# Attention mix in blocks of four key steps, ScalarE drains moved ahead of a block, out projections by chunks of two tiles, and the low parts of the transposed x formed from PSUM

## What is computed

```python
h = layernorm(x) * (1 + ca) + sa
q = h @ Wq.T                                   # 8 heads of 64
kv = h @ Wkv_down.T; k = kv @ Wk_up.T; v = kv @ Wv_up.T
attn = softmax(q @ k.T / 8)
x = x + ga * ((attn @ v) @ Wo.T)
h = layernorm(x) * (1 + cb) + sb
x = x + gb * (h @ weight.T + pooled(h) @ disha)
```

## Time and profile before

| | us |
|---|---|
| median of 3 runs | 3203.18 (3201.83 to 3203.7) |
| the profiled execution, its own time | 3202.91 |
| its span, first to last instruction | 3201.1 |
| PE busy | 3155.7 (99%) |
| POOL busy | 2594.8 (81%) |
| DVE busy | 2198.4 (69%) |
| ACT busy | 1708.8 (53%) |

### The profile page before, as it was taken

How to read it: one execution, slowest core, us unless ns; L and a number is a source line. 1 busy time by engine, 2 the same in 40 slices (tenths; PEclk the granted TensorE clock), 3 DMA queues, 4 the chain that set the end, 5 groups by cost and what they waited for, 6 DMA issues and landing times. The chain is left out here.

```text
span 3201.1 us, 45110 instructions
## 1 busy us (share of the span) xinstructions
PE 3155.7 (99%) x15394; PEld 1916.2 (60%) x15394; DVE 2198.4 (69%) x2530; ACT 1708.8 (53%) x3209; POOL 2594.8 (81%) x1521
## 2 busy tenths in 40 slices
PE   7999999999999999999999999999999999999997
PEld 5555656656566665666666566665666666666555
DVE  6567676776767767677776777767677676776664
ACT  3555555554555555555555555555555455555544
POOL 3888788887878878788887888878878787887786
PEclk9999999999999999999999999999999999999999
DMA  2111111211112111111111111111120121211111
GB/s 82 37 41 60 47 57 34 76 35 47 57 47 67 34 57 54 47 57 44 47 54 56 58 34 54 57 47 57 43 71 31 48 67 38 67 37 48 47 50 41
DMA packets 161252, 162.91 MB, mean 51 GB/s; under 512 B 58112, under 2 KB 109440, under 8 KB 161024
## 3 DMA queue, kind: packets, MB, share of 16 engines
q1 hardware_dynamic: 161024, 160.03, 15.3%
HBM read 74.40 MB, written 17.33 MB: 29 GB/s over the span
## 5 line engine op out<-in xcount | busy, mean ns | idle before, releaser
L962 POOL TENSOR_TENSOR prob_sum<-prob_sum,probs 128x1024 f32<-128x1024 f32 x768 | 1882.6, 2451 | 243.9 <-ACT probs L803 189.4
L1108 DVE TENSOR_REDUCE neg_max<-ps_max 128x1 f32<-128x1024 f32 x1024 | 1247.6, 1220 | 753.9 <-PE ps_max L634 748.0
L803 ACT ACTIVATE probs<-ps_score 128x512 f32<-128x512 f32 x2048 | 1113.3, 598 | 969.2 <-PE ps_score L611 958.3
L588 PE MATMUL ps_mix<-probs,values 128*64 128x512 f32 x4096 | 991.6, 605 | 0.0
L609 PE MATMUL ps_score<-query,key_hi 128*128 128x512 f32 x2048 | 873.8, 427 | 1.1 <-ACT probs L803 1.1
L611 PE MATMUL ps_score<-query_m,key_lo 128*128 128x512 f32 x2048 | 805.1, 393 | 0.0
L634 PE MATMUL ps_max<-key_hi,query 128*128 128x512 f32 x2048 | 640.7, 394 | 5.0 <-DVE neg_max L1108 3.5
L609 PEld LDWEIGHTS ps_score<-query,key_hi 128*128 128x128 f32 x2048 | 384.7, 188 | 326.8 <-issue 247.0
L588 PEld LDWEIGHTS ps_mix<-probs,values 128*64 128x64 f32 x4096 | 248.4, 136 | 477.8 <-issue 477.0
L962 POOL TENSOR_TENSOR prob_sum<-probs 128x1024 f32<-128x1024 f32 x128 | 328.5, 2567 | 209.2 <-ACT probs L803 208.9
L634 PEld LDWEIGHTS ps_max<-key_hi,query 128*128 128x128 f32 x2048 | 383.8, 188 | 96.6 <-DVE neg_max L1108 5.6
(11 more groups left out here) (197 smaller groups left out, 2832.8 us busy)
## 6 DMA issues: line engine op xcount, KB each, us to landing
query_m<-query SPq DMA_DIRECT2D x128, 512.0 KB, 3.2
recip<-recip_scratch SPq DMA_DIRECT2D x254, 128.0 KB, 2.9
x_in<-in_L_attn_x_dram SPq DMA_DIRECT2D x32, 512.0 KB, 3.9
x_mid<-in_L_attn_x_dram SPq DMA_DIRECT2D x64, 256.0 KB, 4.5
out_dram<-x_mid SPq DMA_DIRECT2D x64, 256.0 KB, 2.2
denoms<-recip SPq DMA_DIRECT2D x508, 1.0 KB, 1.7
gates<-gates_scratch SPq DMA_DIRECT2D x16, 256.0 KB, 4.1
query_m<-max_row SPq DMA_DIRECT2D x128, 4.0 KB
```

What stands on the lines that cost most here:

```text
L588: last = nc.tensor.matmul(ps_mix[j * R:j * R + R, :], values[par][:, k, :], probs[:, s % RING, j * HALF:(j + 1) * HALF], start=(k == 0), s ...
L803: nc.scalar.activation(probs[:, s % RING, half * HALF:(half + 1) * HALF], ps_score[half], ACT.Exp, scale=SCALE).then_inc(exps_done, 1)
L962: nc.gpsimd.tensor_tensor(out=total[:, :], in0=before, in1=probs[:, s % RING, :], op=ALU.add).then_inc(adds_done, 1)
L1108: nc.vector.tensor_reduce(neg_max[:, m:m + 1], ps_max[m % 2][:, :], AX_X, ALU.max, negate=True).then_inc(maxima_done, 1)
```

## The change

- MIXED goes from 2 to 4: the mixes stand in blocks of four steps, at the steps with s % 4 == 1, and RING goes from 4 to 6 to hold the probabilities so long. The ring now runs on from batch to batch.
- PLAN is written anew. Pieces whose ACT drain is long stand at s % 4 == 0, pieces that DVE drains and a few transposes at s % 4 == 2. What ACT drains at s % 4 == 2 it drains after the exponentials of the next step. `mixed_hi`, `h2_split` and the high parts of weights stand at s % 4 == 1, the steps with a block. MIX_LAG is 4, and a `denominator` stands at NT*(i+1)+1, `max_row` at STEPS-NT+5+NT*i.
- `out_proj` has 4 pieces of two tiles each.
- For `norm_t` ACT's second pass reads the high part from SBUF and makes shift - high of it, and DVE forms the low part as PSUM * scale + (shift - high) in one SCALAR_TENSOR_TENSOR, which also drains the bank.
- The two copies of `mixed` are replaced by one tile of 11 half rows that consecutive batches share, and the copy-out of a group waits, in groups 2 and 4 to 7, for a `mixed_split` of the batch before.

```diff
-RING = 4
+RING = 6
-SPREAD_LAG, RECIP_LAG, OUT_LAG, BACK_LAG, MIX_LAG = 1, 2, 2, 3, 5
-MIXED = 2
+SPREAD_LAG, RECIP_LAG, OUT_LAG, BACK_LAG, MIX_LAG = 1, 2, 2, 3, 4
+MIXED = 4
-AHEAD_LOAD, AHEAD_STATS, AHEAD_APPLY = 44, (48, 49, 50, 51), 53
-NEXT_LOAD, NEXT_STATS, NEXT_APPLY = 61, (0, 1, 2, 3), 4
+AHEAD_LOAD, AHEAD_STATS, AHEAD_APPLY = 22, (29, 33, 37, 41), 43
+NEXT_LOAD, NEXT_STATS, NEXT_APPLY = 47, (1, 1, 1, 1), 2
-OUT_GATES_LOAD, OUT_GATE, OUT_HI, OUT_LO = 44, 52, 54, (56, 59)
-FFN_GATE, FFN_HI, FFN_LO = (1, 8), (3, 9), (3, 11)
+OUT_GATES_LOAD, OUT_GATE, OUT_HI, OUT_LO = 8, 27, 45, (45, 49)
+FFN_GATE, FFN_HI, FFN_LO = (1, 3), (3, 5), (3, 5)
-    "query": (40, 42, 50, 58, STEPS, STEPS + 2, STEPS + 4, STEPS + 6),
-    "norm_t": (8, 10, 16, 18),
-    "latent": (26, 32),
-    "values_t": (54, 60),
-    "mixed_hi": (9, 16, 24, 40),
-    "mixed_lo": (10, 17, 25, 41),
-    "out_proj": (12, 14, 20, 22, 30, 36, 44, 46),
-    "norm2": (16, 25, 38, 49),
-    "norm2_t": (24, 34, 48, 56),
-    "h2_split": (25, 35, 49, 57),
-    "ffn": (28, 38, 52, 62),
+    "query": (32, 36, 40, 44, 48, 52, STEPS, STEPS + 4),
+    "norm_t": (8, 12, 16, 20),
+    "latent": (24, 28),
+    "values_t": (42, 46),
+    "mixed_hi": (9, 13, 17, 25),
+    "mixed_lo": (9, 13, 17, 25),
+    "out_proj": (10, 14, 22, 30),
+    "norm2": (11, 19, 35, 51),
+    "norm2_t": (18, 34, 50, 56),
+    "h2_split": (21, 37, 53, 57),
+    "ffn": (26, 38, 54, 62),
...
-        "max_row": STEPS - NT + 1 + NT * i,
-        "denominator": NT * (i + 1) + 3,
+        "max_row": STEPS - NT + 5 + NT * i,
+        "denominator": NT * (i + 1) + 1,
...
-                        g, j = divmod(i, CT)
-                        need(pe, mixed_split, CHUNKS * b + g + 1)
+                        need(pe, mixed_split, CHUNKS * b + i + 1)
...
-                    for kind, i, b, w in z.at(s):
+                    late = z.has_c and s % MIXED == 2
+                    for kind, i, b, w in z.at(s - 1) * (z.has_c and s % MIXED == 3) + z.at(s) * (not late):
...
-                            for part, done in ((h_hi[:, f, cols], h_hi_done), (h_whole[:, i % 2, :], side_drained[room])):
-                                nc.scalar.activation(part, side, ACT.Identity,
-                                                     scale=mod1[:, f:f + 1], bias=mod1[:, NF + f:NF + f + 1]).then_inc(done, 1)
+                            nc.scalar.activation(h_hi[:, f, cols], side, ACT.Identity,
+                                                 scale=mod1[:, f:f + 1], bias=shift).then_inc(h_hi_done, 1)
+                            need_alone(act, h_hi_done, 2 * (2 * NF * b + i) + 1)
+                            nc.scalar.activation(h_whole[:, i % 2, :], h_hi[:, f, cols].bitcast(F32), ACT.Identity,
+                                                 scale=-1.0, bias=shift).then_inc(h_hi_done, 1)
...
+                            nc.vector.scalar_tensor_tensor(h_lo[:, f, cols], side, mod1[:, f:f + 1], h_whole[:, i % 2, :],
+                                                           ALU.mult, ALU.add).then_inc(side_drained[room], 1)
```

More of the change, by code:

```diff
@@ L291, in adaln_block @@
         prob_total = recip
-        mixed = [sb(f"mixed{i}", [P, PAIRS, T]) for i in range(2)]
+        mixed = sb("mixed", [P, 2 * PAIRS + 3, HALF])
         mixed_hi = sb("mixed_hi", [P, PAIRS, CT * P], F32R)
@@ L654, in side_work @@
                     elif kind == "latent":
-                        need(pe, h_split, 2 * NF * b + NF * (i + 1))
+                        for f in range(NF):
+                            drained(pe, z, "norm_t", NF * i + f)
                         if first(z):
@@ L689, in side_work @@
                             need(pe, w_out_split, len(OUT_LO) * (b + 1))
-                        g, j = divmod(i, CT)
-                        need(pe, mixed_split, CHUNKS * b + g + 1)
+                        need(pe, mixed_split, CHUNKS * b + i + 1)
                         need(pe, side_drained[room], count)
-                        m_hi, m_lo = mixed_parts(z, g)
+                        m_hi, m_lo = mixed_parts(z, i)
                         products = [(mp, wp, p) for p in range(PAIRS)
                                     for mp, wp in ((m_hi, w_out_hi), (m_lo, w_out_hi), (m_hi, w_out_lo))]
-                        for q, (mp, wp, p) in enumerate(products):
-                            last = nc.tensor.matmul(side[:, 0:D], mp[:, p, j * P:(j + 1) * P],
-                                                    wp[:, p, :], start=(q == 0), stop=(q == len(products) - 1))
+                        for j in range(CT):
+                            for q, (mp, wp, p) in enumerate(products):
+                                pair = PAIRS - 1 - p if (1 - z.par) else p
+                                last = nc.tensor.matmul(side[:, j * D:(j + 1) * D], mp[:, p, j * P:(j + 1) * P],
+                                                        wp[:, pair, :], start=(q == 0), stop=(q == len(products) - 1))
                     elif kind == "norm2_t":
@@ L998, in slot @@
                         need(pool, gates_loaded, 16 * (z.c + 1))
[L999 to L1001 removed]
+                        if not z.has_o:
                             for i in range(4):
@@ L1123, in slot @@
                             hi, lo = mixed_parts(z, g)
-                            nc.vector.tensor_tensor(lo, mixed[1 - z.par][:, :, g * CT * P:(g + 1) * CT * P],
+                            nc.vector.tensor_tensor(lo, mixed_chunk(1 - z.par, g),
                                                     hi.bitcast(F32), ALU.subtract).then_inc(mixed_split, 1)
-                    for kind, i, b, w in z.at(s - 1):
-                        if kind == "norm_t":
-                            need(dve, h_hi_done, 2 * NF * b + i + 1)
-                            drained(dve, z, kind, i)
-                            half, f = divmod(i, NF)
-                            cols = slice(half * HALF, (half + 1) * HALF)
-                            nc.vector.tensor_tensor(h_lo[:, f, cols], h_whole[:, i % 2, :], h_hi[:, f, cols].bitcast(F32),
-                                                    ALU.subtract).then_inc(h_split, 1)
-                    if z.has_n and not first(z) and s in NEXT_STATS:
-                        statistics(z.n, 1, NEXT_STATS.index(s))
+                    for i, t in enumerate(NEXT_STATS):
+                        if z.has_n and not first(z) and s == t:
+                            statistics(z.n, 1, i)
                     for i, t in enumerate(AHEAD_STATS):
```

80 lines of the change are left out of this document (48 added, 32 removed).

## The result

The changed kernel takes **3365.59 us** (3358.11 to 3367.59, 4 runs) against 3203.44 (3201.83 to 3204.41): a ratio of 1.0502, 95% interval 1.0484 to 1.0521. Forecast were 3263 and a range up to 3305. The sign and the two large waits were right, the size was 103 us short.

A forecast was written before the change was run, and what follows sets the result against it. PE was taken to bound the kernel, busy 99% of the span. From 3202.9 us, 90 came off for fewer blocks and 150 were added for new PE waits, giving 3263; the range was 3135 to 3305.

The forecast's parts named there:

- the two large waits: New PE idles a batch: 4.3 us before chunk 1's out projection, and 2.4 twice before the feed-forwards.
- Term 1: Edges of mix blocks on PE: 16 instead of 32 blocks a batch, 0.35 us saved each, -90 us in all.
- Term 2 (a): Second chunk of the out projection, step 14: PE waits 4.3 us for `mixed_lo`, delayed by POOL's additions; 0.8 without the port.
- Term 2 (b): Feed-forward of chunks 1 and 2, steps 38 and 54: PE waits 2.4 us for h2's low part, twice, 4.8.
- Term 2 (c): Denominator of group 0, step 9: PE waits 0.9 us (0 to 1.5) for POOL's chain of additions.
- The clock falls in the waits: Rival: matmuls behind the out projection's 4.3 us wait run at a lower clock, 2.3 more a batch, 3298 us; chance 0.12.
- Terms of nothing: Out projections by two tiles, low part of x from PSUM, and ACT's second pass and later drains: no cost expected.
- at most 15 a run: Bound on the cost if cover for the transposes' drain by ACT at three steps a batch were gone; taken as 0.
- The low part of the transposed x from PSUM: DVE operation with one SBUF tensor, 64 times 0.7 us; DVE was said to have room, so priced at nothing.
- A free port: Rival: the port DVE and POOL share is mostly free, so few waits of PE arise, 3138 us; chance 0.20.
- Only (a) bites: Rival: the feed-forward waits mostly hide and the out projection's wait stays, 3191 us, faster by 0.4%; chance 0.12.
- POOL becomes the bound: Rival: POOL's additions no longer fit a batch of 194, further denominators come late, 120 us more, 3380; chance 0.05.

The follow-up runs named there:

- experiment 1: The changed kernel, with DVE multiplying a group's mix by the reciprocals behind `mixed_lo` of the same step instead of ahead of it: 3280.9 us.
- experiment 3: The changed kernel, with POOL's additions 2 to 7 of each group on 32 of 1024 columns and the first adding ones: 3170.67 us.
- experiment 11: The kernel of experiment 2, with DVE's `w_ffn_lo` at step 6 of a slot instead of step 5: 3177.18 us.
- experiment 4: The changed kernel, with useless PE matmuls ahead of its waits, 14 before the second chunk's out projection and 8 before two feed-forwards: 3320.44 us.
- experiment 5: The kernel of experiment 2, with ACT's two exponentials of a step covering only 256 and 384 of 512 columns: 3140.52 us.
- experiment 2: The changed kernel, with DVE multiplying behind both `mixed_lo` and the low part of h2: 3175.46 us, ratio 0.9907 to the kernel before.
- experiment 7: The kernel before, with only the low part of the transposed x formed from PSUM: 3226.33 us.
- experiment 8: The kernel of experiment 2, with PE's two maxima matmuls ahead of the four score matmuls at steps 0 mod 4: 3232.7 us, ratio 1.0086.

## Why the prediction failed, by its own steps

- **Term 1, fewer blocks, -90:** right. 5.63 a batch against 5.6 forecast, and a block of 3.71 against 3.69. The differences of 0.10 and 0.15 between time stamps in the earlier trace rows were enough to read it.
- **Term 2 (a):** right in place and mechanism; an idle of 3.80 and 3.96 between starts for 4.3, and experiments 1 and 3 show both the wait's worth and its cause. The times came out as in the working: counted from the first score matmul of step 10 in the batch shown above, POOL's norm starts at 6.8 (forecast 6.7), its additions at 9.4 and 11.9 (9.4 and 11.9), the multiplication ends at 14.8 (14.9) and `mixed_lo` at 18.1 (18.4). The multiplication had to wait for one addition in flight, `mixed_lo` for the next.
- **Term 2 (b):** right; 2.38 twice, 5.1 between starts for 4.8.
- **Term 2 (c):** absent in the result, for a reason that the term left out: it took PE as undisturbed up to step 9, and PE had already lost 0.75 behind step 5, where `w_ffn_lo` and the multiplication stand next to each other. The working of (c) was right about POOL (0.84 in experiment 11). The time that it named was lost, under another name.
- **First step that failed: the clock as a rival.** The forecast took (a) and (b) at the full clock and gave 0.12 to "The clock falls in the waits". It does, behind the idle of 3.80 in all fourteen batches, and in all but two of them behind one or both of the 2.38 as well. Nothing in the kernel before shows an idle of this size in mid-batch; but the earlier trace rows showed the fall behind 6.99, and none showed that a shorter idle was harmless. Cost: 3.0 in the batch of the sum, 45 us in all (experiment 4); the rival had 2.3 a batch, for (a) alone. The mean clock of 0.979 is the sign that the prediction itself had named for it.
- **Second: "Terms of nothing", ACT's work.** Between blocks of four, steps now follow each other with nothing but scores and maxima on PE, in 20 places a batch. There the weights of the first scores can't be loaded before the exponentials have freed the bank, so the first two score matmuls start up to 0.08 late each. Before, a block or side work stood in these gaps and hid it. 2.2 in the batch of the sum, 35 us in all (experiment 5). The forecast looked at ACT's share of 107 in 200, which says nothing here: what counts is the time from the last score of one step to the first of the next. The one delay that it priced there, "at most 15 a run", was that of the transposes' drain at three steps a batch; the exponentials at the other steps had no term.
- **Third: the ends of the program.** The terms were priced for 15 like batches. The last slot prepares no batch behind it, so PE has less to do beside each step, and the same waits are longer there: 6.34, 3.28 and 4.48 for 3.80 and 2.38 twice, at a lower clock. Why they are longer was not tested by itself; with DVE's order changed (experiment 2) the last slot is 20 shorter. The beginning and the last slot together are 28 longer; the terms gave them -2.
- **Sum.** Of the missing 102 of the span, 72 lie in fourteen batches, 5.1 each: clock 3.0, late scores 2.2, the single reduction 0.75, less 0.9 by which (a), (b) and (c) together were forecast too high (9.06 measured for 10.0). The other 30 lie in the beginning and the last slot. The forecast and the rival of the clock were written as alternatives, although the fall of the clock follows from the waits that the forecast has. That put the top of the range at 3305.
- **"The low part of the transposed x from PSUM" at nothing:** not borne out where it was tested alone, 22 us in the kernel before (experiment 7). DVE had the room; the bank did not.
- **The rivals.** A free port (3138, 0.20) falls with experiment 3: made free, the port gives back 195 us, so in the changed kernel it was not free. (3170.67 and not 3138, since the late scores remain, 35 us.) "Only (a) bites" falls with experiment 1, in which (a) is gone and 72.0 us ahead of L732 stay. "POOL becomes the bound" falls with the profile: POOL is busy for 76% and PE's L699 matmuls wait for it once, 1.0 us.

What is still open: whether 20 late starts could be hidden by side work placed there (experiment 8 moved maxima and ran into DVE), which was not tried; and what decides at which of the waits of 2.38 the clock falls, which no run shows.

## What to carry to other kernels

When a change makes the order of a shared engine tighter, write that engine's list around each new consumer, and ask of every two neighbours that both use the shared port: which of them is somebody waiting for? The operation that can wait goes last; here that one line, or one lag, was worth between 5 and 6%. A wait on PE is priced with what follows it: the matmuls at the lower clock belong to the same term, not to a rival. And work taken out from between two steps had been covering something; look at what the step behind it needs before it can load its weights.

## What the runs showed of the hardware that was not expected

- Whether an idle of 2.38 in a stream that is otherwise dense is followed by half the granted clock differs from batch to batch of one execution: in the fourteen middle batches of the changed kernel at 13 of 28 places, four times at the earlier one of the batch and nine times at the later; in experiment 1, where the wait of 3.80 is gone, at 19 of 28. Behind the idle of 3.80 the clock fell all 14 times. In the batch of the sum this cost 3.0 more than the idles themselves.
- DVE's delays beside POOL come in turns: the multiplication averaged 1.79 in the changed kernel and 2.43 in experiment 2, for 0.69 when POOL's additions were short. DVE's five operations with two SBUF inputs (the multiplication, `mixed_lo`, the low part of h2, `w_out_lo`, `w_ffn_lo`) take 674 us in all in the changed kernel and 651 in experiment 2, which is 190 faster: what differs most is who waits for them.
- A weight load of the scores that waits for an exponential was not hidden, though the rows of PE show next to no idle time there: its matmul starts up to 0.08 late and the one behind it another 0.08. There were 452 such waits in experiment 2; with 17 left (experiment 5) the kernel was 35 us faster.
